# Layer 1's slot routing: weights by removal among the exponentials, one exponential a chunk, and the attention's run-out in one list of steps with it

## The reference, cut to what matters

```python
# attention of layer 1: 16 heads of 8 features, causal, masked, then
out = attention(x) + x
normalized = (out - mean(out)) / sqrt(var(out) + 1e-8)
x = x + gamma * normalized + beta
# adapter: a low-rank layer of its own for each sequence
x2 = x + einsum('btc,bco->bto', x, base + A @ B.T)
# slots: top 8 of 64 slots for each token
h = gelu(concat(x2, slot_mean) @ w1 + b1)             # exact gelu, 64 wide
route_logits = (h @ w2 + b2) / (abs(tau) + 0.1)       # 64 slots
topk_vals, topk_idx = top_k(route_logits, 8)
alpha = one_hot(topk_idx) weighted by softmax(topk_vals)   # tokens x 64 slots
slot_input = einsum('bts,btd->bsd', alpha, x2) / alpha.sum(over tokens)
# slots: GRU step, attention among the 64 slots, layer norm, slot_values
out = einsum('bts,bsd->btd', alpha, slot_values) @ wo + bo
x = x + out
```

## Time and profile before

| | us |
|---|---|
| median of 3 runs | 1100.55 |
| lowest and highest | 1099.75, 1102.29 |
| the profiled execution | 1102.17 |
| its span, from the first to the last instruction | 1100.9 |
| PE, DVE, ACT, POOL busy in it | 1012.3, 873.0, 798.7, 455.7 |

### The profile page before, as it was taken

One profiled execution on the slowest core, in us unless ns is written; L12 is line 12 of the kernel. 1 busy time (PEld: TensorE's weight loads), 2 busy tenths in 40 slices (PEclk: granted clock), 3 DMA queues, 4 the chain that ended last, 5 costly groups with the idle time before them and its releaser, 6 DMA issues.

```text
span 1100.9 us, 25600 instructions
## 1 busy us (share of the span) xinstructions
PE 1012.3 (92%) x8791; PEld 793.2 (72%) x8791; DVE 873.0 (79%) x3693; ACT 798.7 (73%) x2199; POOL 455.7 (41%) x531
## 2 busy tenths in 40 slices
PE   6999999999999999799799999998898888887788
PEld 5988888888888887432389888877666666655457
DVE  5767878787878797699988998898788888865682
ACT  5877676767676767488878887766777777769864
POOL 1333535353535354238200110027777778861011
PEclk9999999999999999999999999999999999998689
DMA  9000000000000000000000000000000000000002
GB/s 379 1 2 2 2 2 2 1 1 2 2 1 2 2 2 1 1 1 1 0 1 1 1 2 7 4 10 21 21 21 21 21 17 16 12 2 1 1 1 77
DMA packets 8577, 18.32 MB, mean 17 GB/s; under 512 B 1280, under 2 KB 5504, under 8 KB 8064
## 3 DMA queue, kind: packets, MB, share of 16 engines
q1 hardware_dynamic: 8448, 16.69, 4.4%
HBM read 10.39 MB, written 2.10 MB: 11 GB/s over the span
## 4 chain that ended last, share of the span: by engine, by line
PE 61%; DVE 15%; ACT 10%; POOL 8%; issue 4%; DMA 0%; ACTq 0%; DVEq 0%; SPq 0%; POOLq 0%
PE PB L239 6%; PE PB L241 5%; PE PB L240 5%; PE PB L389 5%; PE PB L405 5%; PE PB L372 5%; POOL AR_s L1538 4%; PE PB L334 4%; ACT W L353 3%; PE PB L1056 3%; PE PB L1058 3%; PE PB L1057 3%; PE PB L424 2%; DVE AR_s L1531 2%; DVE W L344 1%
## 5 line engine op out<-in xcount | busy, mean ns | idle before, releaser
L353 ACT ACTIVATE W<-W,small 128x128 f32<-128x128 f32 x512 | 198.7, 390 | 118.2 <-DVE small L344 85.0
L364 POOL TENSOR_TENSOR W<-W,small 128x512 f32<-128x512 f32 x128 | 133.7, 1045 | 241.8 <-DVE small L358 241.8
L239 PE MATMUL PB<-RR_s 128*128 128x256 f32 (+3 forms) x544 | 176.3, 324 | 4.9 <-DVE RR_s L1008 2.5
L241 PE MATMUL PB<-RR_s 128*128 128x256 f32 (+3 forms) x544 | 167.5, 308 | 0.0
L240 PE MATMUL PB<-RR_s 128*128 128x256 f32 (+3 forms) x544 | 167.3, 308 | 0.0
L1538 POOL TENSOR_TENSOR AR_s<-AR_s,small 128x512 f32<-128x512 f32 x128 | 129.8, 1042 | 48.7 <-DVE small L1531 48.6
L1030 ACT ACTIVATE AR_s<-PB,W 128x512 f32<-128x512 f32 (+2 forms) x160 | 100.6, 630 | 28.9 <-PE PB L241 23.2
L344 DVE CUSTOM_DVE_ANT_0 W<-PB,W 128x128 f32<-128x128 f32 x512 | 113.3, 285 | 2.9 <-PE PB L334 0.4
L1044 DVE TENSOR_TENSOR RR_s<-AR_s,RR_s 128x512 fp32r<-128x512 f32 (+2 forms) x160 | 98.5, 621 | 21.1 <-ACT RR_s L1035 17.5
L239 PEld LDWEIGHTS PB<-RR_s 128*128 128x128 f32 x544 | 104.0, 191 | 14.5 <-issue 4.7
L1531 DVE CUSTOM_DVE_ANT_0 AR_s<-PB,W 128x128 f32<-128x128 f32 x512 | 111.5, 285 | 2.0 <-PE PB L1522 1.5
(11 more groups left out here) (353 smaller groups left out, 2387.5 us busy)
## 6 DMA issues: line engine op xcount, KB each, us to landing
W<-in_w SPq DMA_DIRECT2D x1, 5841.0 KB, 24.7
XF<-in_xT SPq DMA_DIRECT2D x4, 512.0 KB, 8.9
out<-XT SPq DMA_DIRECT2D x8, 256.0 KB, 2.3
W<-in_w SPq DMA_DIRECT2D x1, 1088.0 KB, 5.0
W<-in_w SPq DMA_DIRECT2D x1, 1024.0 KB, 7.8
W<-AR_s SPq DMA_DIRECT2D x16, 64.0 KB, 2.1
AR_s<-AR_s SPq DMA_DIRECT2D x16, 64.0 KB, 2.1
QS<-AR_s SPq DMA_DIRECT2D x12, 64.0 KB, 2.1
```

The source lines that it names most:

```text
L239: nc.tensor.matmul(out, lh, rh, start=True, stop=False)
L241: return nc.tensor.matmul(out, lh, rl, start=False, stop=True)
L353: e = nc.scalar.activation(SS[r][:, hl], SS[r][:, hl], ACTF.Exp, bias=mx[r][:, h:h + 1], scale=-1.0, accum_out=rc[r][:, h:h + 1])
L364: nc.gpsimd.tensor_tensor(s3, s3, over(rc[r], 2, [128, 4, 128]), ALU.mult).then_inc(s_nrm, 1)
```

## The change

The weights are made in another way. DVE subtracts the row's maximum from the logits (L1972) and from the 8 largest (L1973) and puts both side by side in one tile of 288 columns; ACT takes one exponential over it, scaled by 1/(abs(tau)+0.1) (L1979). DVE sums the 8 exponentials (L1985), removes them from the 256 by MATCH_REPLACE with zero (L1988), takes the difference (L1993) and multiplies it by the reciprocal of the sum (L1995). The eight exponentials and the four scaled copies of a chunk leave ACT.

The order changes too. The last q of the attention is no longer in the loop but written out, with asides 6 and the first hidden steps between; what follows it is a list `OPENING` that all engines walk ahead of round 0, and `ROUNDS` is dealt anew. Chunk 7's weights are now made between those of 5 and 6, so semaphores count by place in the list (`ROUTED`, `WEIGHED`).

```diff
-        LG = [place(12288 + 256 * c, 256) for c in range(8)]
+        LG = [place(12288 + 288 * c, 288) for c in range(8)]
...
+        OPENING = [("logits", 0), ("add", 6), ("hidden", 3), ("top", 0), ("hidden", 4), ("hidden", 5), ("stats", NB5 - 1),
+                   ("logits", 1), ("hidden", 6), ("top", 1), ("exp", 0), ("apply", 7), ("exp", 1),
...
-        ROUNDS = {0: [("top", 3), ("tokens", 3), ("logits", 5), ("steps", 0), ("alpha", 2), ("alpha", 3), ("top", 4), ("tokens", 4)],
+        ROUNDS = {0: [("steps", 0), ("alpha", 3), ("hidden", 7), ("logits", 5), ("tokens", 3), ("turn", 0), ("top", 5), ("exp", 5)],
...
         def dve_top(c):
-            i, lg7 = c % 2, bank7(("lg", c))[:, 0:256]
-            dve.wait_ge(s_lg, c + 1)
+            n, lg7 = ROUTED.index(c), bank7(("lg", c))[:, 0:256]
+            top8 = m8[n % 2].rearrange("p (b s) -> p b s", b=4)
+            dve.wait_ge(s_lg, n + 1)
             for b in range(4):
-                t = nc.vector.max(m8[i][:, 8 * b:8 * b + 8], lg7[:, b * 64:(b + 1) * 64])
+                t = nc.vector.max(m8[n % 2][:, 8 * b:8 * b + 8], lg7[:, b * 64:(b + 1) * 64])
             t.then_inc(s_r0, 1)
-            dve.wait_ge(s_rex, 2 * (c - 2) + 2)
-            dve.wait_ge(s_r0, 3 * c + 1)
-            nc.vector.tensor_scalar(nmax[i].unsqueeze(2), b4(m8[i])[:, :, 0:1], tinv, -1.0, ALU.mult, ALU.mult).then_inc(s_r0, 1)
+            dve.wait_ge(s_r0, 3 * n + 1)
+            nc.vector.tensor_tensor(b4(LG[c][:, 0:256]), b4(lg7), over(m8[n % 2][:, 0:32:8], 2, [128, 4, 64]), ALU.subtract).then_inc(s_r0, 1)
+            nc.vector.tensor_tensor(b4(LG[c][:, 256:288]), top8, over(m8[n % 2][:, 0:32:8], 2, [128, 4, 8]), ALU.subtract).then_inc(s_r0, 1)
+
+        def act_exp(c):
+            n = ROUTED.index(c)
+            act.wait_ge(s_s7d, 4)
+            act.wait_ge(s_r0, 3 * n + 3)
+            nc.scalar.activation(LG[c], LG[c], ACTF.Exp, scale=tinv).then_inc(s_rex, 1)
+
+        def dve_alpha(c):
+
+            n, al = WEIGHED.index(c), ALPHA[:, c * 256:(c + 1) * 256]
+            dve.wait_ge(s_rex, ROUTED.index(c) + 1)
+            nc.vector.tensor_reduce(sums[n % 2], b4(LG[c][:, 256:288]), AX.X, ALU.add).then_inc(s_r1, 1)
             for b in range(4):
                 sl = slice(b * 64, (b + 1) * 64)
-                t = nc.vector.match_replace(out=MR[c][:, sl], in_to_replace=m8[i][:, 8 * b:8 * b + 8], in_values=lg7[:, sl], imm_value=-1.0e37)
-            t.then_inc(s_r0, 1)
...
+                t = nc.vector.match_replace(out=MR[c][:, sl], in_to_replace=LG[c][:, 256 + 8 * b:264 + 8 * b], in_values=LG[c][:, sl], imm_value=0.0)
+            t.then_inc(s_r1, 1)
+            dve.wait_ge(s_r1, 4 * n + 1)
+            nc.vector.reciprocal(sums[n % 2], sums[n % 2]).then_inc(s_r1, 1)
+            dve.wait_ge(s_r1, 4 * n + 2)
+            nc.vector.tensor_tensor(al, LG[c][:, 0:256], MR[c], ALU.subtract).then_inc(s_r1, 1)
+            dve.wait_ge(s_r1, 4 * n + 4)
+            nc.vector.tensor_tensor(b4(al), b4(al), over(sums[n % 2], 2, [128, 4, 64]), ALU.mult).then_inc(s_ral, 1)
```

More of the change, by code:

```diff
@@ L1478, in plan5 @@
             passes5(("v", 0), 6, s_vt, 1)
[L1479 removed]
+            for q in range(NB5):
                 plan_T5(4 * q - 4)
[L1481 removed]
+                if q >= 2:
                     passes5(("o", q - 2), 4, s_o5, q - 1)
@@ L1491, in plan5 @@
                 plan_T5(4 * q - 1)
-                if 0 <= q - 2 < NB5:
+                if q >= 2:
                     passes5(("oT", q - 2), 6, s_nd, 4 * (q - 2) + 4)
+            for u in range(U - 4, U):
+                plan_T5(u)
+                if u == U - 4:
+                    passes5(("o", NB5 - 2), 4, s_o5, NB5 - 1)
+                if u == U - 3:
+                    plan_aside("gamma", 6)
+            passes5(("oT", NB5 - 2), 6, s_nd, 4 * (NB5 - 2) + 4)
+            plan_aside("select", 6)
+            passes5(("o", NB5 - 1), 4, s_o5, NB5)
+            passes5(("oT", NB5 - 1), 6, s_nd, 4 * (NB5 - 1) + 4)
+            plan_aside("add", 6)
             for what in FINISH.values():
@@ L1847, in pe_order @@
             yield "setup", 0, 0
-            yield "hidden", 0, 0
-            yield "hidden", 1, 0
-            for c in (2, 3, 4, 5, 6):
+            for c in range(3):
                 yield "hidden", c, 0
[L1852 to L1863, removed]
             yield from rounds()
+        ROUTED = [c for what, c, i in rounds() if what == "logits"]
+        WEIGHED = [c for what, c, i in rounds() if what == "alpha"]
         through7, before7 = {}, {}
@@ L1923, in plan7 @@
                     passes7(("at", c), s_att, c + 1)
-                if what == "add":
+                if what == "add" and c == 7:
                     ring7[:], turn7[0] = [0, 1, 2, 3, 4, 5, 6, 7], turn7[0] % 4
@@ L2319, in pe_attend2 @@
                     pe_oT(q - 2)
+            pe_setup()
+            pe_hidden(0)
+            pe_T5(U - 4)
+            pe_PV5(NB5 - 2)
+            pe_hidden(1)
+            pe_T5(U - 3)
+            pe_gamma5(6)
+            pe_T5(U - 2)
+            pe_T5(U - 1)
+            pe_oT(NB5 - 2)
+            pe_select5(6)
+            pe_PV5(NB5 - 1)
             pe_hidden(2)
-            pe_PV5(NB5 - 1)
-            pe_add5(6)
             pe_oT(NB5 - 1)
[L2324 to L2338, removed]
+            parts = {"logits": pe_logits, "hidden": pe_hidden, "tokens": pe_tokens, "turn": pe_turn,
+                     "gamma": pe_gamma5, "select": pe_select5, "add": pe_add5}
             for what, c, i in rounds():
```

109 lines of the change are left out of this document (37 added, 72 removed).

## The result

The changed kernel takes 1092.14 us (median of 4 runs, 1091.34 to 1093.43) against 1100.91 us for the kernel before on the same chip (4 runs, 1099.75 to 1102.29). The ratio is 0.9921, with a 95% interval of 0.9904 to 0.9938: 8.8 us faster. The forecast was 1090.0, in a range of 1083 to 1096.5. The profiled execution took 1091.34 us with a span of 1090.0 us and a granted clock of 0.986. It lies 0.8 us under its median where that of before (1102.17) lay 1.3 above its own, so the spans of the two profiles differ by 10.9 us, not 8.8.

The account below looks back on a forecast made before the run. ACT bounds the stretch from chunk 7's gamma to group 2's step 3, DVE after the change: 34.3 us against 45.1, a 10.8 gain. 1102.17 becomes 1091.4, or 1089.8 against the median, called 1090; range 1083 to 1096.5.

Parts of the forecast that it names:

- ACT sets the pace before, and loses 26 us: From 998.1 to 1043.2 us ACT, busy 40.0 of 45.1 us, is the bound; the change takes 26 us off it.
- DVE pays 3.1 us a chunk, 1.2 and 1.9: DVE's cost of a chunk's weights: "top" 1.2 us and "alpha" 1.9, together 3.1, which is 0.47 more than before.
- The ledger of DVE's stretch, 31.8 us and waits of 2.5: Chunk 7's gamma to group 2's step 3: DVE's queue 31.8 us plus 2.5 of waits, 34.3 against 45.1.
- PE has room at full clock: In the new 34 us stretch PE's work, some 23 us at full clock, fits beside DVE; only just at half.
- Rival 4: PE at half clock becomes the bound from 1000 us on: 3 us slower than before, 1104 us; chance 0.05.
- The run-out, nothing: Attention's run-out up to chunk 7's gamma, expected at 997.6 us against 997.38: nothing counted, between -2 and +3 us.
- Behind it nothing, 57.7 us stay: From 1043.2 us to the end: same work in the same order but two more turns; nothing counted, at most 1 us.
- Rival 1: DVE's stretch keeps waits of 5 us and costs 3.4 a chunk: some 6 us gained, 1094.6; chance 0.22.

Follow-up runs that it names:

- weights_alone: The kernel before with only the new way of making the weights, in the old order: 1089.61 us (ratio 0.9895), and 1089.49 us (0.9891) when run again.
- pe_fed: The changed kernel with three matmuls that nothing reads, where PE waits ahead of step 4 of group 2: 1092.08 us (ratio 0.9915).
- turns_ahead: The changed kernel with the turns of chunks 6 and 7 ahead of the steps of round 5: 1090.93 us (ratio 0.99).
- turns_apply_fed: The changed kernel with turns 6 and 7 ahead of round 5's steps, chunk 7's apply ahead of the last gelu, unread matmuls in three PE waits: 1085.70 us.
- pe_fed3: As pe_fed, with unread matmuls also ahead of chunk 7's gamma (three) and of step 8 of group 3 (two): 1091.69 us (ratio 0.991).

## Why the prediction was right

- *ACT sets the pace before, and loses 26 us*: it lost 24, 40.0 to 16.1 us, with its exponential at the 0.53 us taken; weights_alone shows that this is the gain.
- *DVE pays 3.1 us a chunk, 1.2 and 1.9*: 1.09 and 1.79, 2.88 in all. Over eight "alpha" and six "top" that is 20.9 us instead of 22.4.
- *The ledger of DVE's stretch, 31.8 us and waits of 2.5*: 31.5 us with 0.9 of waits. What is left, 31.5 - 20.9 - 0.9 = 9.7, goes to the slots' steps, select and add, for which 9.4 were put down. The two terms that were too large, by 1.5 and 1.6 us, made the gain 13.6 us and not 10.8.
- *PE has room at full clock*, and its clock stays at 0.70: it had 0.83 over the stretch, and DVE waited for it for 0.9 us. Rival 4, slower by half clock, showed in miniature only: 1.5 us at step 8.
- *The run-out, nothing*: chunk 7's gamma follows chunk 6's after 17.5 us instead of 16.8, 0.7 lost. The start of gamma was forecast at 997.6 and was 997.36, since chunk 6's gamma stood 0.7 us sooner in this profile (979.86 against 980.57); in the changed kernel's second profile it did not (980.45), and chunk 7's gamma came at 997.95. The load ahead of apply was followed by the next instruction after 0.02 us. By an estimate from the drain of 1.38 us that the Trainium skill states (page "ScalarE: Activation LUTs", section "What ACT_TABLE_LOAD costs") gamma would have come that much later, since one load more than before stands ahead of it; the row decides against it.
- *Behind it nothing, 57.7 us stay*: wrong, and the one step that failed. It grew by 2.8 us, over the 2 us that the prediction had named as a sign of being wrong, and with PE at 0.50, as it had said. The argument counted work (two turns of 0.3 us beside a busy DVE) and took the order of steps for the same. It left out what PE's order also decides: when PE is idle, and with it the clock, and who gets which bank. pe_fed takes away 1.5 us of it, turns_ahead 2.1 net.
- Rival 1, *the new order leaves waits*, had the right idea in the wrong place: 0.9 us of waits between 998 and 1029, 2.9 us behind.

The errors of 2.8 us in favour and of 2.8 against cancelled in the profiles (10.9 against the 10.8 forecast). That the profiles agree to 0.1 us is luck; what carries is the sum for DVE's stretch. Against the median the forecast lay 2.1 us low, because it carried the difference of two profiles over to medians.

What stays open: a deal of the banks that sets both v free. The kernel without ties there has step 7 to 8 at 4.9 us where turns_apply_fed has 6.0, so some 1.1 us more is an estimate; it was not tried.

## What to carry to other kernels

Add up the queue of the engine that will set the pace, instruction by instruction: here it gave the new stretch within 3 us. Then look past it: where buffers are dealt in a ring by the order of issue, one instruction moved changes who waits for whom many rows later, so compare the buffer numbers of both orders wherever the work is said to stay. And measure the parts of a change alone: an order made for a full ACT gains 4.9 us with the old weights and costs 3.0 with the new ones.

## What was not expected of the hardware

- Matmuls that nothing reads gained 2.9 us in a kernel in which DVE sets the pace (1088.57 to 1085.70): PE at 0.50 was late to a DVE without slack. Where pe_fed3 had them, ahead of gamma as well, the clock was whole behind gamma but half for 10 us from about 1011 us on, where DVE waited 2.8 us instead of 0.9, so the place decides. The Trainium skill (page "TensorE: Matmul & The Clock Gate", section "HAM oscillation — how this bites in real kernels") advises a loop order in which PE does not wait between its bursts; the runs agree with the aim, and show that PE's waits can also be filled where they stand.
- Four MATCH_REPLACE cost DVE 0.78 us reading SBUF (0.2 a pair of load and replace) as they did from PSUM, and a subtraction of 32 elements 0.18 us against 0.42 for 256.
- An exponential of 288 columns took 0.53 us where one of 64 with columns of bias took 0.41 to 0.45: the eight small ones were short by little for their width, though they had a column operand more, so the two are not quite alike.
